# Attention scores of a two-tile pair computed together in eight strip products, and a new order of steps

## The reference

```
x   = rms_norm(h) ; mixed = where(vm, x @ v_qkv, x @ l_qkv)      # each token takes one of two experts
q,k,v = 16 heads of 16 ; q,k = rotary(q,k)
ctx = softmax(causal(q k^T / 4)) v ; h += where(vm, ctx @ v_dense, ctx @ l_dense)
cq  = rms_norm(h) @ cq_w ; ck,cv = enc @ ckv_w                   # 16 heads of 8, 64 keys, no mask
h  += (softmax(cq ck^T / sqrt(8)) cv) @ cdense_w
mi  = rms_norm(h) ; h += where(vm, mlp(mi; v), mlp(mi; l))       # 688 wide, silu gate
# second layer: attention of h to a memory, a sigmoid gate, rms_norm
```

## Time and profile before

| | |
|---|---|
| three runs | 484.76, 483.12, 484.77 us; median 484.76 us |
| span of the profiled execution, first to last instruction | 474.8 us |
| median less that span | 9.96 us |
| TensorE (PE) busy | 427.1 us, 90% of the span |
| VectorE (DVE) busy | 355.7 us, 75% |
| ScalarE (ACT) busy | 252.7 us, 53% |
| GpSimd (POOL) busy | 134.3 us, 28% |
| DMA | 39.44 MB, 83 GB/s on average |
| mean granted TensorE clock | 0.980 |

### The profile page before, as it was taken

How to read it: one execution, slowest core, us unless ns; L and a number is a source line. 1 busy time by engine, 2 the same in 40 slices (tenths; PEclk the granted TensorE clock), 3 DMA queues, 4 the chain that set the end, 5 groups by cost and what they waited for, 6 DMA issues and landing times.

```text
span 474.8 us, 10858 instructions
## 1 busy us (share of the span) xinstructions
PE 427.1 (90%) x3844; PEld 333.2 (70%) x3844; DVE 355.7 (75%) x810; ACT 252.7 (53%) x706; POOL 134.3 (28%) x246
## 2 busy tenths in 40 slices
PE   1769989899699999999999999999998999799992
PEld 1648767776468679678677777867866688487882
DVE  4888898877887898798699699699784466056575
ACT  3354458667644555556565475564462444466652
POOL 3475213232242032124114204203022100436323
PEclk9998999999989999999999999999998999999997
DMA  7813243864421112102102202111004100213111
GB/s 231 296 58 113 65 150 120 259 220 161 138 68 57 35 31 94 46 24 85 62 12 79 80 1 79 59 33 30 19 23 133 46 23 11 77 46 101 55 43 58
DMA packets 27314, 39.44 MB, mean 83 GB/s; under 512 B 3968, under 2 KB 21376, under 8 KB 27264
## 3 DMA queue, kind: packets, MB, share of 16 engines
q1 hardware_dynamic: 24128, 28.24, 18.4%
q0 software_dynamic: 3136, 10.52, 6.8%
HBM read 25.12 MB, written 13.63 MB: 82 GB/s over the span
## 4 chain that ended last, share of the span: by engine, by line
PE 66%; DVE 18%; ACT 6%; DMA 4%; issue 4%; POOL 1%; SPq 1%; POOLq 0%; ACTq 0%; DVEq 0%
PE b_ps L1653 7%; PE xyz L1540 6%; PE xyz L1499 6%; PE xyz L1526 4%; PE b_ps L1407 4%; DVE E L1144 4%; PE b_ps L1656 3%; PE b_ps L1409 3%; DVE mx L1142 3%; PE b_ps L1408 3%; PE xyz L1738 2%; PE xyz L1407 2%; PE xyz L1409 2%; PE xyz L1408 2%; PE b_ps L1667 2%
## 5 line engine op out<-in xcount | busy, mean ns | idle before, releaser
L1142 DVE TENSOR_REDUCE mx<-xyz 128x8 f32<-128x512 f32 x64 | 43.7, 683 | 5.8 <-PE xyz L1499 5.2
L1499 PE MATMUL xyz<-kT,qT 32*64 32x128 f32 (+1 forms) x768 | 44.1, 328 | 2.3 <-DVE kT L265 0.7
L1144 DVE TENSOR_TENSOR E<-xyz,mx 128x512 f32<-128x512 f32 x64 | 44.3, 691 | 2.2
L1526 PE MATMUL xyz<-cst,E 128*128 128x128 f32 x256 | 36.3, 279 | 3.6 <-ACT E L827 2.7
L259 POOL TENSOR_TENSOR qk<-E 128x256 f32<-128x256 f32 x16 | 14.2, 885 | 87.5 <-DVE E L1124 87.5
L1653 PE MATMUL b_ps<-w_gu_hi,ms_hi 128*128 (+2 forms) x90 | 37.9, 421 | 1.0 <-ACT ms_hi L851 0.6
L863 ACT ACTIVATE th<-b_ps,mrh 128x256 f32<-128x256 f32 (+1 forms) x45 | 20.2, 449 | 33.2 <-PE b_ps L1656 33.2
L1540 PEld LDWEIGHTS xyz<-vb,kT 128*64 128x64 f32 x1024 | 32.4, 138 | 6.9 <-issue 4.8
L1540 PE MATMUL xyz<-vb,kT 128*64 128x18 f32 (+1 forms) x1024 | 34.8, 219 | 2.3 <-DVE kT L1194 1.8
L1526 PEld LDWEIGHTS xyz<-cst,E 128*128 128x128 f32 x256 | 29.2, 142 | 10.3 <-ACT E L827 6.6
L1499 PEld LDWEIGHTS xyz<-kT,qT 32*64 32x64 f32 x768 | 20.7, 134 | 20.8 <-issue 9.0
(11 more groups left out here) (322 smaller groups left out, 1221.5 us busy)
## 6 DMA issues: line engine op xcount, KB each, us to landing
qkv_rows<-qrow SPq DMA_DIRECT2D x13, 384.0 KB, 2.6
xm<-h_rows SPq DMA_DIRECT2D x17, 128.0 KB, 2.0
h_rows<-xm SPq DMA_DIRECT2D x17, 128.0 KB, 1.7
x_sb<-in_x_dram SPq DMA_DIRECT2D x8, 256.0 KB, 2.9
out_dram<-over_gu_lo SPq DMA_DIRECT2D x16, 128.0 KB
xq<-x_rows SPq DMA_DIRECT2D x13, 128.0 KB, 2.8
over_gu_hi<-in_x_dram SPq DMA_DIRECT2D x3, 512.0 KB, 8.2
ctxT_a<-in_ctxT_dram SPq DMA_DIRECT2D x8, 128.0 KB, 3.2
```

The lines of the kernel that those rows point to most:

```text
L1142: dve.tensor_reduce(mx[:, t, heads], s, AX.X, ALU.max).then_inc(max_ready, 1)
L1144: dve.tensor_tensor(E[t][:, b * 512:(b + 1) * 512].rearrange("p (h k) -> p h k", k=SEQ), s, mx[:, t, heads].unsqueeze(2).to_broadcast([P, ...
L1499: last = pe.matmul(xy[t][q, hp, o:o + w], qT[t][rows, c, q], kT[t][rows, (2 * c + b) * w:(2 * c + b + 1) * w], start=not masked, stop=True ...
L1526: last = pe.transpose(xy[t][:, a // 4, (a % 4) * P:(a % 4 + 1) * P], E[t][:, a * P:(a + 1) * P], ident)
```

## The change

- A pair's two tiles are scored together. Phase 0 takes strips 0 and 1 of tile 0 and strips 2 and 3 of tile 1, phase 1 the other strips. Each strip's product is issued for both sequences, so that a chunk of a phase has eight products where there were four, and a pair has two phases for each attention where it had two turns for each tile. The number of products in all is the same.
- The mask is now given strip by strip: eight products of 32 rows and 512 columns before each phase (`strip_masks`, with `mask_q` in place of `ident_q`), where there were two of 64 rows before each tile. A strip masks half of the queries.
- `score_a` and `cscore_a` wait for both tiles (`qT_ready`, `h2_ready`, `kTa_ready`, `kT_ready`, `cqT_ready`, and newly `h1_ready`), `score` and `cscore` wait once per pair.
- The heads come out in another order, so `apply` takes another a for each k.
- Every string of `ORDER` is laid out anew.

```diff
+STRIPS = (((0, 1), (2, 3)), ((2, 3), (0, 1)))
...
+    masked_query = row % RG + RG * (row // SEQ)
+    c[:, C_CAUS:C_CAUS + SEQ] = np.where(np.arange(SEQ) <= masked_query[:, None], 0, NEG)
+    c[:, C_MASK:C_MASK + SEQ] = masked_query[:, None] == np.arange(SEQ)
...
             ("W5", dict(
                 sp="""
-                    m_in:6 m_in:7 m_out:6 load_x:12 load_ca:12 m_out:7""",
+                    load_ca:10 m_in:6 load_x:10 m_out:5 m_in:7 m_in:8 m_out:6 m_out:7""",
...
-            def strip_scores(t, turn, c, chunks, masked, done):
+            def strip_scores(part, c, chunks, masked, turn):
...
-                for strip in range(4):
-                    b, hp = (strip + turn) % 2, strip // 2
-                    q = slice(b * SEQ, (b + 1) * SEQ)
-                    rows = slice(strip * RG, (strip + 1) * RG)
-                    o = (2 * c + strip % 2) * w
-                    last = pe.matmul(xy[t][q, hp, o:o + w], qT[t][rows, c, q], kT[t][rows, (2 * c + b) * w:(2 * c + b + 1) * w],
-                                     start=not masked, stop=True, skip_group_check=True)
...
+                for t in range(TILES):
+                    for strip in STRIPS[part][t]:
+                        rows = slice(strip * RG, (strip + 1) * RG)
+                        o = (2 * c + strip // 2) * w
+                        for b in range(2):
+                            q = slice(b * SEQ, (b + 1) * SEQ)
+                            last = pe.matmul(xy[t][q, strip % 2, o:o + w], qT[t][rows, c, q], kT[t][rows, (2 * c + b) * w:(2 * c + b + 1) * w],
+                                             start=not masked, stop=True, skip_group_check=True)
+                        if c == chunks - 1 and part == 1:
+                            last.then_inc(turn, 1)
...
+            def strip_masks(part):
...
+                            pe.matmul(xy[t][b * SEQ:(b + 1) * SEQ, strip % 2, :], mask_q[rows, :], causal_h[rows, :, :].rearrange("p h k -> p (h k)"),
+                                      start=part == 0, stop=True, skip_group_check=True)
...
-                pe.wait_ge(S["sa_ps"], tl(n, t))
+                pe.wait_ge(S["sa_ps"], n + 1)
+                strip_masks(1)
...
+                pe.wait_ge(S["cqT_ready"], tl(n, 1))
+                pe.wait_ge(S["h1_ready"], tl(n, 1))
+                strip_scores(0, 0, 1, False, S["csa_ps"])
```

More of the change, by code:

```diff
@@ L453, in xattn_kernel @@
-                    cscore:4 cproj:5 gu1:1 cscore_a:5 cscore:5 gu2:1 cprobT:4 hT0:1 cprobT:5 hT1:1 cpv:4 cpv:5 cctxT:4
-                    down:1 cctxT:5 cdense:4 cdense:5""",
+                    miT:0 qkT:4 gu0:0 qkT:5 score_a:4 score:4 gu1:0 gu2:0 probT:4 probT:5 hT0:0 hT1:0 pv:4 pv:5 miT:1
+                    ctxT:4 ctxT:5 down:0 dense:4 dense:5 h1T:4 gu0:1 h1T:5 cproj:4 cproj:5 cscore_a:4 cscore:4 gu1:1 gu2:1
+                    cprobT:4 cprobT:5 hT0:1 hT1:1 cpv:4 cpv:5 down:1 cctxT:4 cctxT:5 qkT:6 cdense:4 cdense:5""",
@@ L471, in xattn_kernel @@
-                    pv:7 hT1:2 ctxT:6 ctxT:7 miT:3 dense:6 down:2 h1T:6 dense:7 cproj:6 gu0:3 cscore_a:6 h1T:7
-                    cscore:6 cproj:7 gu1:3 cscore_a:7 cscore:7 gu2:3 cprobT:6 hT0:3 cprobT:7 hT1:3 cpv:6 cpv:7 cctxT:6
-                    down:3 cctxT:7 cdense:6 cdense:7""",
+                    miT:2 qkT:7 score_a:6 score:6 gu0:2 gu1:2 gu2:2 hT0:2 probT:6 probT:7 pv:6 pv:7 hT1:2 ctxT:6 ctxT:7
+                    down:2 dense:6 miT:3 dense:7 h1T:6 gu0:3 h1T:7 cproj:6 cproj:7 cscore_a:6 cscore:6 gu1:3 cprobT:6
@@ L474, in xattn_kernel @@
+                    gu2:3 cprobT:7 cpv:6 cpv:7 hT0:3 cctxT:6 cctxT:7 hT1:3 qkT:8 cdense:6 cdense:7""",
             )),
@@ L486, in xattn_kernel @@
+                    hT1:4 miT:5 down:4 cscore:8 gu0:5 cscore:9 gu1:5 gu2:5 cprobT:8 cprobT:9 hT0:5 hT1:5 cpv:8 rope:10
+                    cpv:9 rope:11 cdense:8 cdense:9""",
                 pool="""
-                    m_sq:4 get:10 sort:6 sort:7 m_sq:5 get:11 dense:8 dense:9 rope:10 rope:11""",
+                    rope:8 rope:9 sort:6 get:10 get:11 sort:7 m_sq:4 m_sq:5 dense:8 dense:9""",
                 pe="""
-                    qkT:8 qkT:9 score_a:8 score:8 score_a:9 miT:4 score:9 gu0:4 probT:8 gu1:4 probT:9 gu2:4 hT0:4 pv:8
@@ L493, in xattn_kernel @@
+                    cprobT:8 cprobT:9 hT0:5 hT1:5 cpv:8 cpv:9 down:5 miT:6 cctxT:8 cctxT:9 cdense:8 cdense:9""",
             )),
@@ L512, in xattn_kernel @@
+                    ctxT:11 hT1:6 dense:10 dense:11 h1T:10 down:6 h1T:11 miT:7 cproj:10 cproj:11 cscore_a:10 cscore:10
+                    gu0:7 gu1:7 gu2:7 cprobT:10 cprobT:11 hT0:7 hT1:7 cpv:10 cpv:11 down:7 miT:8 cctxT:10 cctxT:11 qkT:12
+                    cdense:10 cdense:11""",
             )),
@@ L531, in xattn_kernel @@
+                    cprobT:12 gu2:9 hT0:9 cprobT:13 hT1:9 cpv:12 cpv:13 down:9 cctxT:12 cctxT:13""",
             )),
@@ L550, in xattn_kernel @@
+                    hT0:10 hT1:10 pv:14 pv:15 miT:11 ctxT:14 ctxT:15 down:10 dense:14 dense:15 h1T:14 gu0:11 h1T:15
+                    cproj:14 cproj:15 cscore_a:14 cscore:14 gu1:11 gu2:11 cprobT:14 cprobT:15 hT0:11 hT1:11 cpv:14 cpv:15
+                    cctxT:14 down:11 cctxT:15 miT:12 cdense:14 cdense:15""",
             )),
```

310 lines of the change are left out of this document (144 added, 166 removed).

## The result

The changed kernel takes 509.41 us (median of four runs, 508.17 to 514.61) where the one before takes 484.76 us (483.12 to 485.05): **1.053 times as long, 95% interval 1.049 to 1.057**. The forecast was 471.5 us.

The account below looks back on a forecast made before the run. TensorE, 90% busy, was taken to bound the kernel if VectorE could feed it. Span 474.8 - 19 + 12 + 2 - 8.3 = 461.5 us, plus 9.96 us between span and median, gave 471.5 us; range 460 to 488 us.

Parts of the forecast that it names:

- The side-by-side products: Score blocks on TensorE: eight products share a round, saving 2.4 us a pair, 19 us for eight pairs.
- the second rival: Score rounds on TensorE: products of one strip don't overlap, 1.0 us saved per pair, time 482.5 us; chance 0.06.
- What it gives back: Between scores and pv or cpv: TensorE waits for VectorE; 12 us for six pairs, 2 us for W0 and W1.
- between nothing and 3 us a pair I take 2.0: W2 to W7: waiting given back per pair, set nearest to the pair worked out; 12 us for the six pairs.
- the order's gains: New order of steps at the start, before pair 2's scores and around MLP tile 12: together 8.3 us saved.
- (a): Pair 0's start: qkT:1 ahead of q_out:4 and other TensorE work to do while waiting; 3 us saved.
- the 36 us that were set as the sign: Sign of being wrong: pair 0 and pair 2 reaching their scores no earlier than 36 and 133 us.
- (b): From cctxT:3 to pair 2's scores: miT:0 and gu0:0 fill the gap, rope precedes cdense; 3 us saved.
- (c): Around 360 us: MLP tile 12's load issued a store earlier, miT:12 ahead of cdense:14; 2.3 us saved.
- the first rival: Between scores and pv or cpv, W2 to W7: VectorE's double load decides, slower, 490.5 us; chance 0.16.
- the third rival: The pairs' waits are covered, each returning 0.5 us instead of 2.0; 462.5 us; chance 0.13.
- the middle: Whole kernel: a weak outcome with some order gains missing, 480 to 487 us; chance 0.16.

Follow-up runs that it names:

- order_only: Kernel before with the new order of steps alone, scores made tile by tile with four products a round; 485.45 us, 1.012 of before on kind A, the quicker chips.
- old_masks: Changed kernel with the mask of the kernel before, four products of 64 rows ahead of phase 0; 484.33 us, 1.014 of before on kind A, the quicker chips.
- after_fourth: The changed kernel itself, unchanged, run on kind A, the quicker chips; 482.52 us, 1.011 of the kernel before.
- after_third: The changed kernel itself, unchanged, run on kind B, the slower chip; 511.28 us, 1.054 of the kernel before.
- after_again: The changed kernel itself, unchanged, run on kind B, the slower chip; 513.23 us, 1.053 of the kernel before.
- sorts_early: Kernel before with GpSimd's indirect transfers moved ahead of m_sq in W2 to W7, beside the self scores; 478.16 us, 1.001 of before on kind A, the quicker chips.

## Why the prediction was wrong

**The side-by-side products: right.** A self block, first mask to first MLP product, takes 218.27 - 216.43 = 1.84 us (predicted 2.3, before 3.57); a cross block 1.44 us (278.07 to 279.51; predicted 1.4). Both sequences of a strip share a round, with 32 records in 0.66 us, so the Trainium skill's rule ("TensorE: Matmul & The Clock Gate", What overlaps and what doesn't) does not decide here, and the second rival is out. The work saved is 2.5 us a pair (2.4 predicted), over the whole execution 427.1 - 410.0 = 17.1 us (19 predicted). What the Trainium skill says in "TensorEngine Tiling (Array Packing)", PSUM Bottleneck, that packing does not speed up the emptying of PSUM, is what the runs show: VectorE's maxima take 684 ns each for 683 before, and joint scoring brings nothing over order_only (1.014 in old_masks and 1.012 on the same chip).

**What it gives back: the mechanism right, the sizes not.** For pair 5, in W5, the count by hand had `pv` 7.95 us after the scores; it begins 266.09 - 258.12 = 7.97 us after. `cpv` was to come at 8.5 us; it comes 288.08 - 279.58 = 8.50 us after. In these two stretches TensorE idles 1.43 and 1.46 us, where it idled 0 and 0.56: 2.3 us given back, 2.35 predicted. VectorE, ScalarE and the banks behave as written (timeline of after_fourth):

```profile
258.11 0.69 DVE L1137 TENSOR_REDUCE mx<-xyz 128x8 f32<-128x512 f32 x1 [0.94 <-PE xyz L1495]
...
261.94 0.43 PE L1659 MATMUL b_ps<-w_gu_hi,ms_hi 128*128 x1 [0.85 <-DVE hid L1223]
...
263.01 1.47 PE L1531 MATMUL xyz<-cst,E 128*128 128x128 f32 x12
...
265.06 0.66 PE L1531 MATMUL xyz<-cst,E 128*128 128x128 f32 x4 [0.58 <-ACT E L790]
...
266.09 0.43 PE L1545 MATMUL xyz<-vb,kT 128*64 128x34 f32 x8
```

**The first step that failed is "between nothing and 3 us a pair I take 2.0": it is 3.65 us of idle time.** W5, the pair worked out, came out as counted. Over pairs 3 to 6 of after_fourth the two stretches give back 2.7 us on average, not 2.0; pair 3 alone 4.0 us. The other 1.0 us lies in the rest of the period, which was costed at nothing: 0.6 us from the start of `pv` to the cross scores, 0.5 us from the start of `cpv` to the next mask. In the four pairs' waits of over 0.1 us those for an exponential (4.2 + 2.8 us) and for `hid` (3.4 us) make about half; the others are for `attT_lo`, `xm`, `kT`, `qT` and `h`, 0.2 to 1.4 us each. The order alone adds 2.0 us of idle time in a pair, 1.3 of them in the same two stretches, although there VectorE gets one tile's scores after the other's. A pair's length says little by itself, since the new order also moves chunks across its borders: pair 5 takes 40.30 us from mask to mask (256.06 to 296.36) for 38.30 (248.25 to 286.55), but with seven chunks of the MLP in place of six, the seventh (`gu0:8`) at 294.81 to 296.36.

**The second step that failed is the order's gains, "together 8.3 us": they are 1.4 us.** (a) Pair 0: the changed kernel starts its self scores at 34.94 us, under the 36 us that were set as the sign; but both tiles are finished at 36.61 us, before at 36.52. TensorE idles 0.6 us less up to there, predicted 3. (b) From pair 1's cross scores to pair 2's self scores it takes 24.2 us (115.8 to 140.0), before 21.7, and pair 2 reaches its scores at 137.07 us, past the 133 us set as the sign of being wrong. `miT:0` and `gu0:0` now lie in this stretch as planned, TensorE is busy for 19.3 us in it instead of 16.2, and its granted clock is 0.80 instead of 0.84; but its idle time falls only from 5.5 to 4.9 us, 0.6 us gained where 3 were predicted. Its timeline:

```profile
131.89 0.69 DVE L1117 TENSOR_TENSOR E<-qkv,rope 128x512 f32<-128x512 f32 x1 [2.90 <-DMA qkv<-qkv_rows,slot_q]
...
133.63 0.42 DVE L1203 TENSOR_TENSOR ms_lo<-b_ps,ms_hi 128x256 fp32r<-128x256 f32 x1
...
134.10 1.22 PE L1662 MATMUL b_ps<-w_gu_hi,ms_lo 128*128 x2 [2.36 <-DVE ms_lo L1203]
135.12 0.63 PE L1477 MATMUL xyz<-cst,qk 128*128 128x128 f32 x2
```

`rope:5` waits 2.90 us for its gathered tile, `ms_lo` of `miT:0` stands behind it, `gu0:0` waits for `ms_lo`, and `qkT:5` stands behind `gu0:0`. The work that was to fill the gap is tied to the wait that makes it. (c) In the kernel before, the new MID and L1 gain 1.7 us by the medians, for 2.3 predicted. In the changed kernel nothing of it is seen: from pair 7's cross scores to the end it takes 122.0 us, before 121.8.

**The sum on kind A.** TensorE's idle time by stretch, from the two traces of kind A:

| stretch | before | changed | difference | predicted |
|---|---|---|---|---|
| start to pair 0's self scores | 16.3 us | 15.7 us | -0.6 | -3 (a) |
| to pair 1's cross scores | 5.0 | 8.8 | +3.8 | +2 |
| to pair 2's self scores | 5.5 | 4.9 | -0.6 | -3 (b) |
| to pair 7's self scores | 5.8 | 24.5 | +18.7 | +12 with the next |
| to pair 7's cross scores | 0.4 | 2.1 | +1.7 | |
| to the end | 14.7 | 14.5 | -0.2 | -2.3 (c) |
| together | 47.7 | 70.5 | +22.8 | +5.7 |

Less the 17.1 us of work this gives +5.7 us, 480.5 for 474.8 us, where the forecast had 461.5. Of the 19.0 us between the two, 8.4 are the pairs' waits (20.4 for 12), 1.8 those of pairs 0 and 1, 6.9 the order's missing gains and 1.9 the work. With the first step right the span would have been 2.7 us shorter than before, with the second right 1.2 us; it took both to turn the sign. On the prediction's scale 1.1% slower is 490 us, just what the first rival gave, but by luck: its condition, a mean wait of over 2.1 us in each of the twelve attentions, was not met (20.4 / 12 = 1.7), and it counted on the order's 8.3 us. The shares of the chances are a trifle off too: the forecast, the third rival and a fifth of the middle add up to 0.71, not 0.73.

**What no step had.** The other 4.2% exist on kind B alone: the changed kernel is 511.28 - 482.52 = 28.8 us slower there than on A, the one before 7 us. The idle brackets before the second phase add up to 21.3 us in the changed kernel (18.4 in after_third); the remainder fits the clock (mean 0.948 for 0.973: about 27 us more at the lower level, in which rows took 1.5 to 1.6 times as long, so 9 to 10 us; an estimate from the two means). By the runs on B this is shown: late ends of over 0.6 us are found only where indirect transfers run beside the self scores, in every program that ran there (though not every overlap costs so much: pair 2 of after_again and after_third has under 0.5 us, pair 1 of the kernel before none); they go where the transfers are held back; they come with the new order alone. The amount moved does not tell the kinds apart: in pair 4 it was 214 GB/s in the gap on kind B and 214 GB/s at the same place in after_fourth (217.3 to 221.0 us), where TensorE was busy for 3.59 of 3.70 us. The prediction has no term for what runs beside the scores on GpSimd. It could have seen that the transfers moved: `rope` of a pair went from the stage before into its own, so that `sort` no longer follows `m_sq`. It could not have seen a price, since the trace it had was from a chip where there is none; the gap of 9.96 us between median and span was a hint that was read as launch and end, which take 2.2 us.

What stays open: why the two kinds differ, and whether there are more chips like the one of kind B in the experiments; what more transfers beside the scores cost there in the kernel before (sorts_early never ran on it); whether it is GpSimd's work on the descriptors or the rows they move that counts; and why strip products end late by whole microseconds while the full products issued behind them go on.

## What to carry to other kernels

Where a change moves steps, cost every stretch of the period and every pair, by its idle time and not by its length: here the one pair that was worked out came out right (2.3 us for 2.35), and the six pairs together were wrong by 8.4 us. Work put in to cover a wait covers nothing if its own input comes from behind that wait. And before times are set against a trace, compare the run's time with its own span: here the usual difference was 1.7 to 2.3 us, and the 9.96 us meant that the two came from different chips.
